# Three routing batches in the first expert layer, earlier starts at four joints, and no memset ahead of GpSimd's indirect transfers

## The reference

```python
x = x + gnn0(layernorm(x))      # relu of two gated adjacency products and a gated loop
x = x + ffn0(layernorm(x))      # H = gelu(x @ W1 + b1) (512 wide); e = argmax(H @ Wg + bg);
                                # softmax prob[e] * (H @ Wd[e] + bd[e]), 8 experts, one each
x = x + gnn1(layernorm(x))      # two adjacency layers, then LSTMs over windows of p = 1..4 nodes
x = x + ffn1(layernorm(x))      # router, top 2 of 8; silu(x @ w1[e]) * (x @ w3[e]) @ w2[e], gated sum
```

## Time and profile before

| | us |
|---|---|
| median of 3 runs | 1212.13 (1201.58 to 1217.56) |
| the profiled execution | 1216.61 |
| its span, first to last instruction | 1214.9 |
| its mean granted TensorE clock | 0.946 |

### The profile page before, as it was taken

One profiled execution on the slowest core, in us unless ns is written; L12 is line 12 of the kernel. 1 busy time (PEld: TensorE's weight loads), 2 busy tenths in 40 slices (PEclk: granted clock), 3 DMA queues, 4 the chain that ended last, 5 costly groups with the idle time before them and its releaser, 6 DMA issues.

```text
span 1214.9 us, 18080 instructions
## 1 busy us (share of the span) xinstructions
PE 1031.3 (85%) x5428; PEld 719.9 (59%) x5429; DVE 601.2 (49%) x1811; ACT 519.9 (43%) x967; POOL 526.8 (43%) x1138
## 2 busy tenths in 40 slices
PE   4789985889988899998998997889897888888881
PEld 2334431567666644653883364359787788888780
DVE  7855883211055265655755752437465533323354
ACT  5466853334332486664347563543532222222120
POOL 6922276640643520000220077515526566666671
PEclk9698997899999999999999999889998999999995
DMA  9930001232332100000000021145545565747957
GB/s 278 363 146 1 1 31 57 75 91 69 99 83 81 35 18 0 1 1 0 1 1 1 3 94 49 34 117 158 170 137 163 173 228 175 240 165 243 331 166 238
DMA packets 98151, 131.14 MB, mean 108 GB/s; under 512 B 12130, under 2 KB 67986, under 8 KB 97170
## 3 DMA queue, kind: packets, MB, share of 16 engines
q1 hardware_dynamic: 85522, 104.11, 26.9%
q0 software_dynamic: 12544, 25.98, 6.4%
HBM read 85.47 MB, written 44.58 MB: 107 GB/s over the span
## 4 chain that ended last, share of the span: by engine, by line
PE 63%; DVE 14%; another core or an unknown queue 7%; issue 6%; ACT 6%; POOL 3%; DMA 1%; DVEq 0%; ACTq 0%; POOLq 0%; SPq 0%
PE bank L1307 13%; PE bank L1333 13%; PE bank L1314 8%; PE bank L1343 5%; PE bank L1066 4%; PE bank L1187 4%; PE bank L1227 3%; PE bank L1255 2%; PE bank L1092 2%; DVE sb_R L2098 2%; PE bank L1244 1%; PE bank L1216 1%; DVE sb_R L1467 1%; PE bank L1236 1%
## 5 line engine op out<-in xcount | busy, mean ns | idle before, releaser
L1307 PE MATMUL bank<-sb_R,sb_wih_sb 128*128 128x512 f32 (+2 forms) x504 | 202.2, 552 | 15.9 <-DVE sb_R L1991 10.7
L919 ACT ACTIVATE sb_R<-bank,sb_lb_sb 128x512 f32<-128x512 f32 (+2 forms) x252 | 152.1, 634 | 88.4 <-PE bank L1314 68.3
L2098 DVE TENSOR_TENSOR sb_R<-sb_R,bank 114x384 f32<-114x384 f32 x136 | 75.1, 552 | 201.2 <-PE bank L1343 111.9
L952 ACT ACTIVATE sb_R<-bank 114x384 f32<-114x384 f32 x136 | 65.7, 491 | 254.2 <-PE bank L1333 161.4
L682 POOL DMA_INDIRECT expert_out<-sb_R,sb_slot_row x136 | 131.8, 969 | 94.5 <-issue 44.2
L1307 PEld LDWEIGHTS bank<-sb_R,sb_wih_sb 128*128 128x128 f32 x504 | 96.4, 193 | 114.4 <-issue 82.8
L640 POOL MEMSET sb_pause_p<- 128x1 f32 x392 | 44.0, 112 | 222.0 <-DVE sb_dest_i L1653 84.5
L1343 PE MATMUL bank<-sb_BIG,sb_R 114*128 x816 | 117.8, 281 | 3.8 <-DVE sb_R L2033 3.4
L1333 PE MATMUL bank<-sb_xt,sb_BIG 128*114 128x128 f32 x816 | 105.5, 281 | 18.0 <-DVE sb_R L2098 9.5
L1314 PE MATMUL bank<-sb_R,sb_whh_sb 128*128 128x512 f32 (+2 forms) x288 | 111.2, 529 | 0.9 <-DVE sb_R L1994 0.9
L1333 PEld LDWEIGHTS bank<-sb_xt,sb_BIG 128*114 128x114 f32 x816 | 97.4, 184 | 22.2 <-issue 19.1
(11 more groups left out here) (326 smaller groups left out, 1751.6 us busy)
## 6 DMA issues: line engine op xcount, KB each, us to landing
sb_BIG<-up_t SPq DMA_DIRECT2D x68, 342.0 KB
sb_wih_sb<-up_t SPq DMA_DIRECT2D x34, 342.0 KB
sb_whh_sb<-up_t SPq DMA_DIRECT2D x34, 342.0 KB
sb_XS<-expert_in SPq DMA_DIRECT2D x17, 528.0 KB
expert_in<-sb_R SPq DMA_DIRECT2D x17, 512.0 KB, 6.0
sb_R<-expert_out SPq DMA_DIRECT2D x7, 1024.0 KB, 7.1
sorted_in<-sb_R SPq DMA_DIRECT2D x9, 512.0 KB, 5.4
sb_XS<-sorted_in SPq DMA_DIRECT2D x18, 256.0 KB
```

Of the source, the lines that this page charges most:

```text
L919: act.activation(gb[s][k][:, 0:c], bank[4 * s + k][:, 0:c], funcs[k], bias=lb_sb[:, (p - 1) * GATES + k:(p - 1) * GATES + k + 1]).then_inc ...
L952: act.activation(sl[j % 2][0:HC, :], bank[2 + 2 * (j % 2)][0:HC, 0:KU * P], ACT.Silu).then_inc(d2_silu, 1)
L1307: mm = pe.matmul(bank[4 * s + k][:, 0:c].rearrange("p (w b) -> p w b", b=GH), wih_sb[:, p - 1, k * P:(k + 1) * P], xin, start=True, stop=( ...
L2098: dve.tensor_tensor(hm[j % 2][0:HC, :], sl[j % 2][0:HC, :], bank[3 + 2 * (j % 2)][0:HC, 0:KU * P], ALU.mult).then_inc(d2_m, 1)
```

## The change

1. **Three batches in layer 1.** `PARTS` are tiles 0 to 23, 24 to 47 and 48 to 63. The first is chosen in turns 3 and 4, the second in turns 6 and 7, the third after turn 7, with its ranks on PE behind the first hidden layer of b2 instead of ahead of b2. The place arithmetic is that which the last layer already uses (`OpenPlaces`), extended by a jump over eight open slots that come in the middle (`skip`). Groups 0 to 3 of b2 need the first batch, 4 to 7 the second, the rest the third. The gathers come in three parts.
2. **Waits.** `g_norm` of the first two steps of each half of layer 2 moves ahead of the last bias addition of b2 and into the last two LSTM steps; PE's waits at both starts move behind the adjacency pipeline or two steps into it; the routing of the last layer writes one small table column later; the reads at the end come in three parts (blocks 0 to 3, 4 and 5, 6 to 8) at groups 13 and 15 and at the end, with their additions at other slots.
3. **`pause()` is removed** from all 392 places. Pacing waits stay; those of the scatters of layer 1 are new.

```diff
-    NSLOT0 = -(-(NTILE + E - 1) // 4) * 4
-    CLOSED0 = (NH - E + 1) // 4 * 4
-    OPEN0 = NH + E - 1
+    NSLOT0 = NTILE + E
+    PARTS = ((0, 3 * NH // 4), (3 * NH // 4, 3 * NH // 2), (3 * NH // 2, NTILE))
+    KNOWN0 = ((3 * NH // 4 - E + 1) // 4 * 4, (3 * NH // 2 - 2 * (E - 1)) // 4 * 4)
+    OPEN0 = KNOWN0[1]
...
-        B2A, B2B = CLOSED0 // 4, -(-OPEN0 // 4)
+        B2_READY = (KNOWN0[0] // 4, KNOWN0[1] // 4)
+        GATHERS = ((0, 3 * NH // 4, B2_READY[1] + E // 4), (3 * NH // 4, NH, 3 * NH // 8 + E // 4), (NH, NTILE, NB2))
+        CHOICE_TURNS = {PARTS[0][1] // 8: 0, PARTS[1][1] // 8: 1}
...
-        HALF_GROUPS = (READY[1] + 1, ND2)
-        D3_LOAD = ND2 - 3
-        D3_ADD = 8 * (ND2 - 2)
+        D3_GROUPS = (READY[1] + 1, 3 * NH // 8 + 1, ND2)
+        D3_LOAD_AT = (ND2 - 4, ND2 - 2)
+        D3_ADD_AT = {8 * ND2 - 20 + 2 * n: (n // 2, n % 2) for n in range(8)}
+        D3_ADD_AT |= {8 * ND2 - 5: (4, 0), 8 * ND2 - 3: (4, 1), 8 * ND2 - 2: (5, 0), 8 * ND2 - 1: (5, 1)}
...
-            sp.wait_ge(s_scat[0][0], 16 * NH)
+            sp.wait_ge(s_scat[0][0], 16 * (PARTS[0][1] - PARTS[0][0]))
             sp.wait_ge(a_t1, NA)
             b2_load(0, 0)
             b2_load(1, 1)
-            run_pairs(sp, 2, B2A, b2_both)
-            sp.wait_ge(s_scat[0][1], 16 * NH)
-            run_pairs(sp, B2A, NB2, b2_both)
+            run_pairs(sp, 2, B2_READY[0], b2_both)
+            sp.wait_ge(s_scat[0][1], 16 * (PARTS[1][1] - PARTS[1][0]))
+            run_pairs(sp, B2_READY[0], B2_READY[1], b2_both)
+            sp.wait_ge(s_scat[0][2], 16 * (PARTS[2][1] - PARTS[2][0]))
+            run_pairs(sp, B2_READY[1], NB2, b2_both)
...
-            def pause():
-                step(pool.memset(pause_p[:, :], 0.0))
...
+                    if b == 0:
+                        pool.wait_ge(rb.h, KH * NG // 2 + 7 + 3 * i // 4)
+                    elif b == 1 and i < 10:
+                        pool.wait_ge(rb.h, KH * NG - 9 + i)
+                    elif b == 1:
+                        pool.wait_ge(b2_h, 1 + 5 * (i - 10) // 8)
+                    else:
+                        pool.wait_ge(b2_h, 10 + 7 * i // 8)
...
-                    if half == 0:
-                        pool.wait_ge(b2_h, KH * (B2B + 1) + 5 * i // 8)
+                    if t < NH:
+                        pool.wait_ge(b2_h, min(KH * (done + 1) + 5 * (t - lo) // 8, KH * NB2))
...
             def rows_home(i):
-                pause()
                 pool.wait_ge(d2_yo, i + 1)
...
             b1_part_copy(NG - 1)
-            route_copies(0, rb, 1)
-            route_exp(0, rb, 1)
             copy_xt(r2, 0, 0)
...
                 hidden(r2, g, u)
                 if first:
-                    pe.wait_ge(rb.ranks_sb, HALVES)
-                    pe.wait_ge(rb.tiles, HALVES)
+                    pe.wait_ge(rb.tiles, 2)
                 if not last:
                     transposes4(g + 1, 1 - u, r2, xs, (b2_in[1 - u], 16 * (k + (1 if u == 0 else 2))))
+                if first:
+                    rank(0, rb, 2, 7)
...
-            pe.wait_ge(b2_yo, NB2)
             for half in range(HALVES):
                 if half > 0:
-                    pe.wait_ge(l_act, half * gates_before[NL])
+                    pe.wait_ge(l_act, gates_before[NL - 1])
...
+            in_b[1].weights(0)
+            in_b[1].table()
             b1_store(NG - 2)
             b1_store(NG - 1)
-            in_b[1].begin()
+            in_b[2].begin()
...
+                if isinstance(g, int) and g == NB2 - 1:
+                    g_norm(0, 0)
+                    g_norm(0, 1)
...
+                    if half == 0 and n >= NL - 2:
+                        g_norm(1, n - (NL - 2))
```

More of the change, by code:

```diff
@@ L657, in scatter, with scatter_d @@
+            def scatter_d():
+                pool.wait_ge(rd.dest, 1)
+                for t in range(NH):
+                    pool.wait_ge(l_h, NL + SCATTER_STEP + (NL - 1 - SCATTER_STEP) * t // NH)
+                    for k in range(2):
                         pool.indirect_dma_start(
-                            out=rows, out_offset=bass.IndirectOffsetOnAxis(ap=dest_i[:, k, t:t + 1], axis=0),
-                            in_=src[:, t - half * NH, :], in_offset=None).then_inc(s_scat[layer][half], 16)
@@ L1656, in _, with __init__ @@
             class OpenPlaces(Places):
+                def __init__(self, layer, b, r, K, tiles, staged, open_row, te, table_of, most, known, skip):
+                    super().__init__(layer, b, r, K, tiles, staged)
+                    self.open_row, self.te, self.table_of, self.most = open_row, te, table_of, most
+                    self.known, self.skip = known, skip
                 def counts(self, part):
-                    w, b, nt = self.w, self.b, self.nt
-                    start, count, n, end, low, high, edge, base, rest, over, edge2, high2 = (small[:, i, :] for i in range(12))
+                    w, b, nt, skip = self.w, self.b, self.nt, self.skip
+                    start, count, n, end, low, high, edge, base, rest, over, edge2, high2, turn = (
+                        small[:, i, :] for i in range(13))
                     opened, room, past = (carry[:, i, :] for i in range(3))
@@ L1844, in _, with table_b, table_d @@
[L1844 to L1846 removed]
+            def table_b(slot):
+                return OPEN0 if slot == NTILE else slot + E if slot >= OPEN0 else slot
+            def table_d(slot):
+                return slot
+            assert NH <= NL - 3 and HALVES == 2
@@ L1850, in _ @@
                     b1_store(2 * p - 2)
-                if p == NA // HALVES:
+                if p in CHOICE_TURNS:
                     b1_store(2 * p - 1)
-                    in_b[0].begin()
-                if p == NA // HALVES + 1:
-                    in_b[0].counts()
-                    in_b[0].places()
-                    in_b[0].rows(0)
+                    in_b[CHOICE_TURNS[p]].begin()
+                if p - 1 in CHOICE_TURNS:
+                    chosen = in_b[CHOICE_TURNS[p - 1]]
+                    for part in range(3):
+                        chosen.counts(part)
+                    chosen.places()
+                    chosen.rows(0)
+                    if CHOICE_TURNS[p - 1] == 1:
+                        chosen.carries()
                 if p + 1 < NA:
@@ L1865, in _ @@
                     a_sum(p + 2)
-                if p > 1 and p != NA // HALVES:
+                if p > 1 and p not in CHOICE_TURNS:
                     b1_store(2 * p - 1)
@@ L1916, in b2_dve @@
                     b3_finish(0)
-            in_b[1].counts()
-            in_b[1].places()
-            in_b[1].rows(0)
-            in_b[1].table()
-            in_b[1].weights(0)
-            sweep(dve, 0, NB2, b2_dve, 2, behind=5)
-            def g_norm(half, i):
-                n = half * NGH + i
-                if n >= 2:
-                    dve.wait_ge(c1_ax, n - 1)
-                for j in range(4):
-                    q = 4 * n + j
-                    ins = dve.tensor_scalar(xn[i % 2][:, j, :], X[:, q, :], MEAN[:, q:q + 1], RSTD[:, q:q + 1],
-                                            ALU.subtract, ALU.mult)
-                ins.then_inc(c1_xn, 1)
+            in_b[2].counts(0)
+            in_b[2].counts(1)
+            in_b[2].places()
+            in_b[2].rows(0)
+            in_b[2].weights(0)
+            in_b[2].table()
+            sweep(dve, 0, NB2, b2_dve, 2, behind=5)
             def g_bias0(half, i):
```

313 lines of the change are left out of this document (144 added, 169 removed).

## The result

The changed kernel takes 1216.0 us (median of 20 runs), the kernel before 1212.0 (20 runs): ratio 1.009, 95% interval 1.007 to 1.012. Every ratio here leaves out executions more than 1.5% above the fastest of the same kernel, here five of before's 20, with which the medians stand at 1.003. The difference is inside the 2% that this measurement can tell from no change. The forecast was 1143. The profiled execution of after has a span of 1213.9, 1.0 under that of before.

The account below looks back on a forecast made before the run. It took PE's late signals during POOL's runs of indirect transfers, paced near a slot's length, to cost D2 and b2 time. Gains less 8 at slot 112 summed to -70 from 1214.9: 1145, as median 1143; range 1095 to 1232.

Parts of the forecast that it names:

- The loss and its place: D2 loses 93 us and b2 22, PE stands idle 8.38 in the LSTM; PE's signals come late in POOL's runs.
- 392 transfers are 0.39 us shorter each, 153 us of POOL's time: All indirect transfers: without memset and semaphore each is 0.39 us shorter, 153 us of POOL's time, none by itself on the path.
- the term of -40: D2: removing the pauses was to save 40 us, taken between estimates of 27 and some 60.
- b2's -5: b2: removing the pauses was to save 5 us of late signals.
- The cycle of POOL as the slot's bound: D2: 1.6 transfers of 1.35 us plus wakes make 2.47 us, close to the 2.7 a slot takes.
- Rival C: D2's and b2's runs: the gap was PE's window, so removal costs 0.75 us per transfer, 1279 in all; chance 0.19.
- Start of b2, -10.9: b2's start: with the first batch loaded early, PE starts near 201.6 instead of 212.52; gain 10.9 us, bound 5.9.
- The clock term: b2's first hidden layer: after a shorter idle it may run at the full clock; gain 3.1 us, bound 0.
- Second LSTM, -8: Second LSTM: POOL keeps up without the pauses and PE's 8.38 us of idle go; gain 8, bound 0.
- Layer 2, -5.6: Starts of layer 2's halves: moving `g_norm` earlier gains 1.7 and 3.9 us, together 5.6, bound 2.
- The end, -5.4: Final reads: three blocks instead of five remain after the last home transfer, last additions 4.8 us; gain 5.4.
- Slot 112, +8 (0 to 12): D2, slot 112: group 14's weights wait behind four 1 MB reads, so PE idles 8 us, bounds 0 and 12.

Follow-up runs that it names:

- a_pause_scat: Changed kernel, first final reads behind group 14's weights, pauses back only ahead of layer 1's and the second LSTM's 64 scatters each: 1178.5 us, 0.971 of before, late chip.

## Why the prediction was wrong, point by point

**The loss and its place: right.** I read 93 us lost in D2, 22 in b2 and 8.4 in the second LSTM as PE's signals coming late in POOL's runs, with 2.1 us for a slot undisturbed. The prompt chips show the same program with slots of 2.09 and without that loss in b2 and the LSTM. Of D2's 93 some 47 are lateness. Another 33 are waits at the routing batches (slots 8 to 24 take 57 us on a prompt chip, not 34) and at the final reads (slots 112 to 120 take 25.7, not 16.7), and 12 are the start, from 811.6 to the first gate.

**"392 transfers are 0.39 us shorter each, 153 us of POOL's time": the step that failed.** They are 0.09 shorter, 35 us. I added up memset, semaphore and transfer and took the first two away; the gap between two transfers was there without them. With 0.09 my own proportion (0.09/1.35) would have given 6 us in D2 instead of 27, and that much came in the steady slots: 138.2 us instead of 143.5 for slots 48 to 104. The hold in slots 8 to 16 took 6.8 back. So the term of -40 measured about 0, as -5 and +7. Of b2's -5 nothing shows in the old order (158.6 us without pauses, 157.3 with).

**The cycle of POOL as the slot's bound: wrong.** The nearness of 2.47 and 2.7 was a coincidence; on prompt chips POOL keeps the same cycle of 1.35 and slots take 2.09.

**Rival C, the gap as PE's window: right in kind, wrong in place and size.** I placed it in D2 and b2 at 0.75 us a transfer, 84 us. It is in layer 1 (b2's start 214 instead of 205 to 207, a comparison across chips) and the second LSTM (175.7 instead of 159.4 on one chip), some 20 us together, and in one place of D2, 6 to 7 us. I had weighed the ten scatters behind the choice, but not the 22 ahead of it, which the new waits join into one run.

**Start of b2, -10.9.** 200.95 on a prompt chip against my 201.6; on the late one +1.7. My bound, a gain of 5.9, allowed for part of DVE's chain and not for a hold ahead of the whole of it. The clock term was right: the first hidden layer takes 3.70 us at 215.50 instead of 6.75.

**Second LSTM, -8.** Measured +0.8: it hung on the pauses, the other way round.

**Layer 2, -5.6.** 3.7 on the late chip and 4.5 on the prompt one; PE now waits 3.05 us instead of 4.21 at the first half.

**The end, -5.4.** The last additions take 5.14 us (forecast 4.8; 10.18 before); the end is 2.3 shorter on the late chip and 6.0 on the prompt one.

**Slot 112, +8 (0 to 12).** 11.38 us, for the reason told, near the upper end. The Trainium skill, DMA: Bandwidth & Descriptors, "Two DMAs through the same engine are not ordered", has descriptors of one queue start in order, by which I made it 12, and the trace agrees with that better than with my 8. Its price depends on when SP gets free: 10.6 on a prompt chip, 19.0 there with pauses.

**Sum.** With the terms as measured in the two profiled executions: +1.7 (start) - 4.9 (b2, the clock in it) - 3.7 (layer 2) + 0.8 (second LSTM) + 0.5 (the stretch up to D2) + 6.9 (D2) - 2.3 (end) = -1.0, where I had -70. Of D2's 6.9 the stall is 11.4 and the hold at slots 8 to 16 is 6.8; the steady slots give back 5.3 and those from 112 on 8, and some 2 are spread over the rest. Of the 69 us between forecast and measurement 38.9 are D2's (the 40 of pauses above all), 12.6 b2's start, 8.8 the LSTM, 3.2 b2, 3.1 the end, 1.9 layer 2, 0.5 the stretch. The medians stand 4 us apart the other way, which is within what single executions spread on a late chip (before 1198 to 1225).

**What stays open.** Why PE's signals come late on some chips and not on others, and why a memset and a gap of 0.28 us in which POOL waits for its semaphore let them out where 0.30 us of "issue" do not: that they do is shown by the second LSTM with and without pauses on one chip, and by slots 8 to 16 in seven traces, why is not shown. Nor did a run on a late chip take the indirect transfers away. The second LSTM stalled in the old order with pauses too (172.4) and not in the new one, twice; no run tells why. a_pause_scat met no prompt chip; the kernels beside it, with all pauses and with none, take 0.989 and 0.984 to 0.987 there.

## What to carry to other kernels

Price an instruction that you take out of a repeated sequence by the distance between its neighbours with and without it, not by its own duration and semaphore: here 0.09 us were left of 0.39. When two edits meet in one change, such as pauses out and waits loosened, measure them apart: without pauses the old waits left runs of 12 and ten transfers in layer 1, the loosened ones a run of 22, and the missing pause cost more in the new order than in the old. A stage whose total does not move can still hold two effects, as D2 does; compare it in parts. Put no read that waits for a slow producer ahead of weights with little lead in one queue: moving it back by one group gave 0.4 to 1.3%. The version that beats both kernels on late chips is the new order with late reads and pauses ahead of the two scatter runs only, at 0.971, or ahead of all transfers, at 0.965 and on a prompt chip 0.989; the intervals of the two overlap.

## What the hardware showed that I had not expected

Chips of one type differ by 7% on the same program (1137 against 1215), in three and three of those met, at the same time in every stage in which POOL issues few or none (265.9 us against 267.1). A share of the chain under "another core or an unknown queue" on a kernel of one core, 7% here and none on a prompt chip, was the mark of it. And holds of ACT of 7.0, 9.9 and 11.8 us were seen inside runs of 22 and 28 transfers (30 and 37 us), each ending between 2 us before and 3 after the run's end; a run of five was enough for DVE to get PE's signal 2.5 us late.
